# Relative queries brought by DMA, and a later place for the second batch's expert tiles

## The reference

```python
# block 1: causal attention, 16 heads of 8, with relative positions
q, k, v = split_heads(x @ Wq + bq), split_heads(x @ Wk + bk), split_heads(x @ Wv + bv)
rel = jnp.einsum('bhid,pd->bhip', q, rel_key)              # 256 distances
rel_idx = jnp.clip(j - i + p - 1, 0, p - 1)
bias = jnp.take_along_axis(rel, jnp.broadcast_to(rel_idx[None, None], (b, h, s, s)), axis=3)
logits = jnp.where(causal[None, None], (scores + bias) * scale, -jnp.inf)
out = (softmax(logits) @ v) @ Wo + bo
# block 2: silu(x wg) * (x wu), hidden 384, then wd, weights as int32 / 127
# block 3: quaternion attention, 16 heads of 8, all 512 keys, normed q and k, four small products
#          per projection, plus 0.1 * mean(sin(J)) on the scores
# block 4: 8 experts of 512, gelu, the two best of a softmax over the experts, weighted sum
```

## Time and profile before

| | |
|---|---|
| median of three runs | 947.34 us |
| the profiled execution | 946.77 us, of which the span of its instructions is 944.7 us |
| mean granted clock of PE | 0.949 of full speed |
| PE | 764.6 us, 81% |
| PE weight loads (beside PE) | 548.1 us |
| ACT | 495.8 us, 52% |
| DVE | 449.9 us, 48% |
| POOL | 178.9 us, 19% |

### The profile page before, as it was taken

How to read it: one execution, slowest core, us unless ns; L and a number is a source line. 1 busy time by engine, 2 the same in 40 slices (tenths; PEclk the granted TensorE clock), 3 DMA queues, 4 the chain that set the end, 5 groups by cost and what they waited for, 6 DMA issues and landing times.

```text
span 944.7 us, 21455 instructions
## 1 busy us (share of the span) xinstructions
PE 764.6 (81%) x8384; PEld 548.1 (58%) x8384; DVE 449.9 (48%) x1528; ACT 495.8 (52%) x1013; POOL 178.9 (19%) x306
## 2 busy tenths in 40 slices
PE   1677888798987899988999987678786787489994
PEld 0466777576765576675565753255553563267773
DVE  3154543665545364435345552474765535521416
ACT  0335555457754659765658753548554554233321
POOL 4200101000010000010000003033324382115411
PEclk9999999899997999998999998989998998879998
DMA  3500110001300001200000410110411120011011
GB/s 99 178 2 2 68 61 2 1 3 45 114 2 12 1 13 48 89 25 12 2 13 2 130 31 20 44 29 26 154 46 45 42 61 23 6 29 46 23 34 37
DMA packets 36440, 38.29 MB, mean 41 GB/s; under 512 B 8982, under 2 KB 26220, under 8 KB 36212
## 3 DMA queue, kind: packets, MB, share of 16 engines
q1 hardware_dynamic: 34548, 33.65, 11.8%
q0 software_dynamic: 1536, 3.15, 1.1%
q10 hardware_dynamic: 256, 0.13, 0.0%
HBM read 19.87 MB, written 16.91 MB: 39 GB/s over the span
## 4 chain that ended last, share of the span: by engine, by line
PE 54%; DVE 17%; issue 14%; ACT 10%; ACTq 1%; another core or an unknown queue 1%; DMA 1%; POOL 1%; SPq 1%; POOLq 0%; DVEq 0%
PE ps L1696 5%; PE ps L1545 5%; PE ps L1566 4%; PE ps L1711 4%; PE ps L1771 4%; PE ps L1473 3%; PE ps L1579 3%; PE ps L1548 3%; PE ps L1783 3%; ACT late L908 3%; ACT probsT L758 3%; PE ps L1542 2%; PE ps L1646 2%; PE ps L1794 2%; DVE stats L1017 2%
## 5 line engine op out<-in xcount | busy, mean ns | idle before, releaser
L908 ACT ACTIVATE late<-ps,j_bias 128x512 f32<-128x512 f32 x256 | 174.7, 694 | 152.6 <-PE ps L1696 131.3
L1171 DVE TENSOR_REDUCE neg_max<-ps 128x2 f32<-128x32 f32 (+31 forms) x128 | 90.5, 707 | 166.7 <-PE ps L1551 161.5
L1696 PE MATMUL ps<-q_heads,k_parts 128*128 128x512 f32 x256 | 135.1, 542 | 20.4 <-ACT late L908 17.6
L758 ACT ACTIVATE probsT<-ps 128x128 f32<-128x128 f32 (+3 forms) x256 | 98.1, 438 | 81.0 <-PE ps L1566 67.3
L834 ACT ACTIVATE probs<-ps,neg_max 128x16 f32<-128x16 f32 (+31 forms) x256 | 110.5, 495 | 32.2 <-DVE neg_max L1171 32.2
L627 POOL TENSOR_TENSOR q_wide<-qT,eighth_mask 128x1024 f32<-128x1024 f32 x16 | 31.2, 1950 | 368.4 <-PE ps L1551 285.7
L1566 PE MATMUL ps<-ident,probs 128*128 128x128 f32 x640 | 95.6, 280 | 2.1 <-ACT probs L834 2.1
L1696 PEld LDWEIGHTS ps<-q_heads,k_parts 128*128 128x128 f32 x256 | 49.8, 200 | 72.3 <-ACT late L908 47.5
L1545 PE MATMUL ps<-kT_two,q_wide 64*64 64x262 f32 (+16 forms) x1024 | 72.7, 347 | 15.8 <-ACT probsT L758 10.3
L1566 PEld LDWEIGHTS ps<-ident,probs 128*128 128x128 f32 x640 | 74.9, 142 | 18.2 <-issue 8.2
L1711 PE MATMUL ps<-late,v_two 128*9 128x512 f32 x512 | 73.0, 636 | 9.5 <-DVE late L1157 8.3
(11 more groups left out here) (265 smaller groups left out, 1245.7 us busy)
## 6 DMA issues: line engine op xcount, KB each, us to landing
k_parts<-k_half SPq DMA_DIRECT2D x16, 256.0 KB, 3.3
q_parts<-q_half SPq DMA_DIRECT2D x16, 256.0 KB, 3.5
k_parts<-k_parts SPq DMA_DIRECT2D x16, 256.0 KB, 3.1
q_heads<-q_parts SPq DMA_DIRECT2D x64, 64.0 KB, 2.1
x_by_expert<-q_heads SPq DMA_DIRECT2D x3, 960.0 KB, 7.6
probsT<-x_by_expert SPq DMA_DIRECT2D x45, 64.0 KB
y_by_expert<-probsT SPq DMA_DIRECT2D x45, 64.0 KB
late<-in_L_ffn_w_dram SPq DMA_DIRECT2D x1, 2048.0 KB
```

The lines of the kernel that those rows point to most:

```text
L758: return nc.scalar.activation(o, i, ACT.Copy)
L908: nc.scalar.activation(head_probs[:, i % SLOTS, :], ps[:, banks[i % len(banks)], :], ACT.Exp, bias=j_bias[:]).then_inc(e2_ready.sem, 1)
L1171: nc.vector.tensor_reduce(neg_max[:, n % 4, :], ps[:, k:k + OCT, 0:QS * (n + 1)], axis=AXX, op=ALU.max, negate=True).then_inc(max_ready.se ...
L1696: mm(ps[:, banks[i % R], :], k_parts[:, hg, kc * P:(kc + 1) * P], q_heads[:, hg % 2, g, :], start=True, stop=True).then_inc(s2_ready.sem, 1)
```

## The change

**q by token, then by DMA.** The eight-fold product, its weights and DVE's 128 masked reads go. Instead H has one piece more: PE forms q with tokens on partitions (four products of 128 x 128 x 128, columns ordered octet, d, head), and DVE scales it and adds the bias in one instruction of 512 columns into `q_nat`. SP stores `q_nat` to DRAM, and for each tile brings it to `q_rel` with eight DMAs, one for each token of a block of 8: 16 rows x 16 blocks x 8 heads. Everything else in `q_rel` is zero, which POOL writes once. Scores of a tile wait for the eight DMAs. R is now one piece a tile.

**The order within tiles.** For that, 8 heads lie next to each other in `q_rel`, `q_wide` and `ahead_pick`, and the tokens of a block one step apart, where it was the other way round. The scores and `probs` have their rows in that order too, so ACT's copies of the turned rows now take elements in another order: what was written in runs of 8 tokens is written one element at a time, 64 elements apart, in `probsT`, whose two outer dimensions change places. The rows of `toep` are reordered, and 8 DMAs of ACT fill it instead of 16, with the sine for block 3 in the middle.

**Loads.** The bias for all partitions is one DMA instead of 16. The loads of w1, w2 and block 3's weights move from SP's head behind the first R pieces, and the zeroing of `x_by_expert` to the 46th piece of W.

**The plan.** H begins at half step 45 instead of 50 and has 12 pieces; R stands at 52 of the round before and at 0, 14 and 30. X of batch 1 begins at 13 instead of 10. N has two pieces more, and POOL's scatter stands two pieces later in it. The sums C fall into four pieces for DVE instead of two; in DVE's first sum the wait for the gather, the products, the additions, the statistics and the rest part ways.

```diff
@@ plan
-            if a < B:
-                put(r, 0, "R", a, 4)
-                put(r, 13 + late, "R", a, 4)
-                put(r, 34 + late, "R", a, 4)
+                put(r, 0, "R", a, 1)
+                put(r, 14, "R", a, 1)
+                put(r, 30, "R", a, 1)
...
-                put(r, 50, "H", a + 1, 10)
-                put(r, 60, "R", a + 1, 4)
+                put(r, 45, "H", a + 1, 12)
+                put(r, 52, "R", a + 1, 1)
...
-                put(r, 52, "N", 0, 18)
+                put(r, 52, "N", 0, 20)
...
-                put(r, 10, "X", 1, NX - 4, 3)
+                put(r, 13, "X", 1, NX - 4, 3)
                 put(r, 33, "C", 0, 4, 3)
-                put(r, 50, "C", 0, 2)
-        yield from [("H", 0)] * 10 + [("R", 0)] * 4
+                put(r, 50, "C", 0, 4)
+        yield from [("H", 0)] * 6 + [("R", 0)] + [("H", 0)] * 6
...
-            yield from [("C", LAST - 2)] * (2, 2, 1, 1, 0, 0, 0, 0)[k]
-            yield from [("C", LAST - 1)] * (0, 0, 0, 0, 0, 4, 1, 1)[k]
+            yield from [("C", LAST - 2)] * (2, 2, 2, 2, 0, 0, 0, 0)[k]
+            yield from [("C", LAST - 1)] * (0, 0, 0, 0, 0, 4, 2, 2)[k]
@@ SP
-            sp.dma_start(w1_in, w1.rearrange("(m p) e d -> p m e d", p=P)).then_inc(ld_moe, 16)
-            sp.dma_start(w2_in[:], w2).then_inc(ld_moe, 16)
...
+            def head(b):
+                for _ in range(5):
+                    yield
+                sp.wait_ge(b7_free, fill_no["H", b, 4] + 1)
+                sp.dma_start(q_nat_dram[b].rearrange("t n i e c -> (n i) t (e c)"), q_nat[:]).then_inc(q_nat_out.sem, 16)
+                yield
+
+            def relative(b):
+
+                if b == 0:
+                    sp.wait_ge(q_rel_zero, 1)
+                sp.wait_ge(q_nat_out.sem, q_nat_out.at(b + 1, 0))
+                for t in range(T):
+                    if b * T + t >= 2:
+                        sp.wait_ge(scores_ready.sem, scores_ready.at(b, SPT * (t - 1)))
+                    for i in range(QB):
+                        sp.dma_start(q_rel[i:P:QB, t % 2, :, i, :],
+                                     q_nat_dram[b][t, :, i, :, :].rearrange("n e c -> e n c")).then_inc(q_rel_in[t % 2], 16)
+                    yield
@@ POOL, norm, ahead of the scatter
-                for _ in range(2):
+                for _ in range(4):
                     yield
@@ copy_pT
-            copy(probsT[:, 0:c, o, :, (n % SPT) * QB:(n % SPT + 1) * QB],
-                 ps[:, turned_bank(b, n, o), 0:c * P].rearrange("p (c r i) -> p c r i", r=2 * HO, i=QB)
+            copy(probsT[:, o, 0:c, :, (n % SPT) * QB:(n % SPT + 1) * QB].rearrange("p c (z h) i -> p (c z) i h", z=2),
+                 ps[:, turned_bank(b, n, o), 0:c * P].rearrange("p (k i h) -> p k i h", i=QB, h=HO)
@@ ACT
-            for r in range(0, P, RR):
-                for i in range(QB):
-                    c = S - QB - NREL + 1 + i
-                    rows = slice(r + i * D, r + (i + 1) * D)
-                    act.dma_start(toep[rows, c:c + NREL], rel_rows[rows, :]).then_inc(toep_dma, 16)
+            for i in range(QB):
+                if i == QB // 2:
+                    act.wait_ge(j_ready, 1)
+                    nc.scalar.activation(j_turn, j_row, ACT.Sin, accum_out=j_sum[:]).then_inc(j_ready, 1)
+                    nc.scalar.preload_act_table_set("exp_and_others")
+                c = S - QB - NREL + 1 + i
+                act.dma_start(toep[i:P:QB, c:c + NREL], rel_rows[i:P:QB, :]).then_inc(toep_dma, 16)
@@ DVE, head; the stage R is gone
+                full("H", b, 4)
+                if b:
+                    dve.wait_ge(q_nat_out.sem, q_nat_out.at(b, 0))
+                nc.vector.scalar_tensor_tensor(
+                    out=q_nat[:], in0=token_tiles(B7), scalar=SCALE, op0=ALU.mult, op1=ALU.add,
+                    in1=q_bias_nat[:].rearrange("p o d c -> p (o d c)").unsqueeze(1).broadcast_to([P, T, P])
+                    ).then_inc(b7_free, 1)
@@ PE, head; the stage R is gone
+                by_distance = w_qkvo[:, 0, :].rearrange("e (o c d) -> e o d c", o=OCT, d=D)
+                for t in range(T):
+                    last = mm(bank7[:, t * P:(t + 1) * P], head_T[:, t * P:(t + 1) * P], by_distance,
+                              start=True, stop=True)
+                last.then_inc(b7_full, 1)
@@ PE, scores
-                    pe.wait_ge(b7_free, fill_no["R", b, 4 * t + 2] + 1)
+                    pe.wait_ge(q_rel_in[t % 2], 16 * QB * (b * T // 2 + t // 2 + 1))
```

176 lines of the change are left out of this document (83 added, 93 removed).

## The result

The changed kernel takes 971.62 us (median of 4 runs, 968.30 to 977.09) against 946.40 us; the ratio is 1.0269, 95% interval 1.0211 to 1.0326. It is slower, where I forecast 909 us, and outside my range.

A forecast was written before the change was run, and what follows sets the result against it. PE, busy 764.6 of 944.7 us, was taken as the engine to look at, with place deciding. Start 10, rounds 20 and expert stages 8 made 38 us: span 906.7, time 909 us, forecast alone 897 to 921, range 894 to 951.

The forecast's parts named there:

- The copies: ACT's copies of the turned probabilities into probsT, now written 64 elements apart: extra cost taken as zero.
- the shares of the rounds: At p ns more an element in ACT's copies, round 0 passes on 20.5p, round 1 7p, rounds 2 and 3 12p each.
- rival A: ACT's hopping writes cost: 960 us at 1 ns an element, 952 at 0.84, 924 to 947 at 0.3 to 0.75; chance 0.35.
- The start: Up to PE's first transpose of w1: 49.0 instead of 58.98 us, 10 us saved; first scores 10.1 us earlier.
- The expert stages: Three waits of PE shortened by the later plan steps: 3, 2 and 3.5 us, together 8.5, taken as 8.
- The three waits: PE's single waits in the expert stages of 4.39, 4.21 and 4.86 us, before batch 1's tile, behind batch 2's scatter, before L1711.
- The rounds: Attention rounds: 24.6 us back from removed relative products, less 3.9 for three q-by-token products; 20 us taken.
- the cover of k and q: SP's queue: k and q of the FFN's output behind the query DMAs still arrive before PE's first use; cost nothing.
- B: Query DMAs' small runs are slow, 6.6 us a tile instead of hiding in the issues: 917 us; chance 0.07.
- D: q_rel arrives 9 us late for every batch's first tile, 36 us in all: 945 us; chance 0.02.
- Rival C: Freed time in the rounds turns into waits for ACT's and DVE's loops; at half of the 20 us, 919; chance 0.06.

The follow-up runs named there:

- e12: None of the four blocks computed: copies and products with hops measured by themselves on otherwise idle engines, in one execution of 154.76 us.
- e5: Changed kernel, but PE's turning writes its 128 columns 8 apart into the bank and ACT's copy is the old one: 928.83 us, 0.9801 of the kernel before.
- e3: Kernel before, with only the later steps of the plan (batch 1's tiles, POOL's scatter, sums in four pieces) as changed: 938.54 us, 0.9919.
- e10: e5 with the loads of w1 and w2 issued at their old place in SP's queue, ahead of q by token: 923.79 us, 0.9828.
- e8: Kernel before with one of four relative products and one of DVE's four masked reads in each half tile: 925.51 us, 0.9776.
- e6: Changed kernel, but PE turns against an identity with columns ordered by head, and ACT's copy is the old one: 928.37 us, 0.9806.

## Why the prediction was wrong, step by step

- **The copies, the step that failed.** I took an extra of zero ("the nearest row, the same copy"), though no row showed such a write; it is 0.92 ns an element. That is 43 us (971.6 less 928.8) of the miss of 63 (971.6 less 909). The mechanism, the point from which it decides (0.75 ns) and the shares of the rounds stood in rival A, whose time at p = 0.84, 952, and at p = 1, 960, are too low because the base of 909 was too low. The row that I leaned on hops once in eight elements; e12 shows that this says nothing about a hop at each element.
- **The start: right where it ends.** I forecast 10 us to the first transpose of w1, and 9.7 were measured. The loads of w1 and w2 set that point, and both their issue (34.83) and the 14.5 us that they take came as forecast. The way there did not: the scores came 11.9 us earlier and not 10.1 (issues were dearer at 0.65 us, ACT's freed time larger), PE then needed 15.2 us and not 10.8 (in e5, with the fast copies, still 14.5, as PE is at half speed), and the wait for w1 swallowed the difference.
- **The expert stages: the size right, the waits in part.** I forecast 8 us; e3 has 7.0, and in e5's trace the stretch behind round 3 is 8.0 shorter. One trace says little here: the same instructions take 376.4 us in e5 and 370.2 in e10. The three waits went, but two others came, so that the size came out is partly luck.
- **The rounds, the second step that failed: 20 us forecast, 1.5 in e5.** I moved H five half steps earlier at no cost but that to SP's queue, and its products fell ahead of the turning: with q by token's product (2.1 us instead of 1.3; L1476, 421 ns a record, as it reads Wq 8 apart) that is 5.6, 2.0 and 3.9 us in rounds 0 to 2, where I had 3.9 for the three. Behind the transpose of w1, e5's round 0 is 5.1 us longer than before (99.5 against 94.4), where I had about 3 less. Besides those 5.6 us it loses 2.4 up to its tenth step, since PE, whose first instructions run at half speed, is at full speed in e5 from about 61 us instead of 53 (four transposes of w1 take 1.11 us at 55.93; the clock column shows 1.00 there all the same). It gains 0.6 in the middle, where by e8 the removed products mostly stood beside waits for ACT, and 2.3 at the last scores. Round 1 was 6.5 us shorter, as forecast, so its 2.0 were made up elsewhere. Round 2 was 3.4 us longer where I had some 6 less, and 9.1 longer than e8's 142.2: 2.9 us are the cover of k and q that I cost at nothing, 2.3 the clock behind that wait, and 3.9 the projections. Round 3 was 3.4 us shorter and not 5.1.
- **Rivals B and D** each had a grain: the queue's own time, not the small runs' transfer (landing took 2.4 us), made the one late hand-over. Rival C is what the middle of round 0 shows. The clock was in none of my terms: the mean granted clock of the changed kernel's profiled execution is 0.920 (0.929 to 0.931 in its other three runs) against 0.949. By how much that lengthened the run beside the copies was not measured apart.

## What to carry to other kernels

When a change alters the order of a layout, price each copy by the innermost step on both its sides: if no row has that step, measure it alone before summing the rest, since the zero was two thirds of my miss. Look for the engine on which the permutation is free, here the write of PE's turning. And a line's share in the chain is worth its time only in the stretches where no other loop is as long: read it round by round. The same goes for work that is only moved: a product behind the turning filled a wait and cost nothing, and ahead of it the same product cost its full length and more.

## What the runs showed of the hardware

- ACT and DVE copy 512 columns of f32 from the bank, writing single elements 64 apart, in 1,061 and 1,011 ns; pairs in 629 and 692, runs of four in 597 and 691. Reading 8 apart and writing in order costs nothing (597 ns on ACT, e12).
- PE reads its moving f32 operand 1 or 2 elements apart in 275 ns a record of 128 columns, and 4 or 8 apart in 404 to 412; its writes 8 apart stay at 275 (e12).
- Turning against a permuted identity gives permuted columns at 283 ns a record on the mean of e6, where the hopping write of e5 has 284 and the kernel before 280.
- In e5, after a pause of 2.9 us, PE's granted clock was 0.50 from 257.3 to 262 us, and 128 products took 6.0 us where they take 3.7 at full clock.
